# Two networks and a mixture of experts: transposes between the layers, smaller one-hot pieces, a shared last stage

## What is computed

```python
logits = xf @ w_router                       # N = 8192 rows, 8 experts
gate, eidx = jax.lax.top_k(softmax(logits), 2)
gate = gate / gate.sum(-1)
pos = cumsum(one_hot(eidx)) - 1              # place of a row in its expert, kept if < C
h = relu(expert_in @ w1[e] + b1[e])          # C = 768 rows an expert, 256 -> 1024
expert_out = h @ w2[e] + b2[e]               # 1024 -> 256
y = sum over the two choices of expert_out * gate
x = layernorm(x + y)
```

## Time and profile before

| what | us |
|---|---|
| median of 3 runs | 2886.46 |
| the profiled execution, in all | 2887.04 |
| its span | 2885.2 |
| `ssm_phase`, end of its last copy to the first load of `moe_phase` | about 2391.9 |
| from there to the end | about 493 |

### The profile page before, as it was taken

The page is one execution under the profiler, slowest core; times in us unless marked ns, Lnnn a source line. Parts: engine busy times, 40 slices in busy tenths (PEclk is TensorE's granted clock), DMA queues, the critical chain, the costliest instruction groups (busy, mean ns, idle before and its releaser), DMA issues. The chain is left out here.

```text
span 2885.2 us, 51759 instructions
## 1 busy us (share of the span) xinstructions
PE 2642.1 (92%) x16812; PEld 2403.8 (83%) x16812; DVE 2434.5 (84%) x3452; ACT 2274.4 (79%) x5161; POOL 2155.9 (75%) x2239
## 2 busy tenths in 40 slices
PE   5899999999999999999999999999999884899992
PEld 4899999999999999999999999999999874576761
DVE  1999999999999999999999999999999986112113
ACT  6999999999999999999999999999999922111113
POOL 1788888888888888888888888888888862423315
PEclk8999999999999999999999999999999986999996
DMA  1222222222222222222232222222222212323216
GB/s 59 67 75 79 78 71 79 78 69 82 71 80 77 75 76 78 73 80 70 77 81 72 79 77 75 77 78 73 80 70 79 72 51 85 81 59 99 60 43 244
DMA packets 153973, 225.73 MB, mean 78 GB/s; under 512 B 46056, under 2 KB 92776, under 8 KB 152552
## 3 DMA queue, kind: packets, MB, share of 16 engines
q1 hardware_dynamic: 131208, 188.98, 22.3%
q0 software_dynamic: 9216, 12.59, 2.5%
q10 hardware_dynamic: 13280, 20.86, 2.1%
HBM read 189.26 MB, written 33.05 MB: 77 GB/s over the span
## 5 line engine op out<-in xcount | busy, mean ns | idle before, releaser
L642 POOL TENSOR_TENSOR H<-H,CB 128x640 f32<-128x640 f32 x832 | 1236.1, 1499 | 224.0 <-DVE H L479 223.9
L479 DVE TENSOR_TENSOR_SCAN H<-DA,PM 128x704 f32<-128x704 f32 x832 | 1317.1, 1604 | 1.3 <-ACT DA L276 1.3
L394 ACT ACTIVATE DA<-DT,SM 128x160 f32<-128x160 f32 x3328 | 1115.9, 424 | 1.5 <-POOL DT L610 0.3
L664 PE MATMUL YB<-H,ID 128*128 128x160 f32 x6656 | 1050.5, 310 | 0.2 <-POOL H L642 0.2
L664 PEld LDWEIGHTS YB<-H,ID 128*128 128x128 f32 x6656 | 989.0, 192 | 16.4 <-issue 11.2
L454 DVE TENSOR_TENSOR PM<-PM,BB 128x640 f32<-128x640 f32 x832 | 678.7, 816 | 5.8 <-DMA BB<-Bd 0.7
L276 ACT ACTIVATE DA<-DA 128x2560 f32<-128x2560 f32 x208 | 485.4, 2334 | 1.7
L1121 POOL DMA_INDIRECT YA<-YS,IG x48 | 75.2, 1566 | 239.9 <-ACT YS L944 228.4
L621 POOL TENSOR_TENSOR FC<-SN,HALF 128x4 f32<-128x4 f32 x206 | 212.4, 1031 | 31.2 <-DVE SN L485 23.2
L765 PE MATMUL PZ<-WO,Z 128*80 128x256 f32 x832 | 188.5, 380 | 0.1
L1177 PE MATMUL PE<-XTE,W 128*128 128x384 f32 x512 | 169.1, 492 | 10.1 <-issue 9.2
(11 more groups left out here) (164 smaller groups left out, 3993.7 us busy)
## 6 DMA issues: line engine op xcount, KB each, us to landing
BB<-Bd SPq DMA_DIRECT2D x208, 320.0 KB, 3.4
CB<-Cd SPq DMA_DIRECT2D x208, 320.0 KB, 3.3
W<-in_w ACTq DMA_DIRECT2D x16, 1024.0 KB
XT<-in_xT SPq DMA_DIRECT2D x52, 160.0 KB, 2.2
XR<-in_xp SPq DMA_DIRECT2D x416, 20.0 KB
X2d<-VV SPq DMA_DIRECT2D x416, 20.0 KB
YA<-VV SPq DMA_DIRECT2D x416, 20.0 KB
HI<-YA SPq DMA_DIRECT2D x6, 1024.0 KB, 9.9
```

The costliest lines, as they stand in the source:

```text
L394: eng.activation(DA[:, c0:c0 + 2, :, a, m, 1:11].rearrange("p c b t -> p b c t"), DT[:, j % 2, a].rearrange("p b (c t) -> p b c t", c=2), ...
L479: eng.tensor_tensor_scan(H[:, q % 3, u], a0, DBX(u), 0.0, ALU.mult, ALU.add).then_inc(s_scan, 1)
L642: eng.tensor_tensor(h, h, cb, ALU.mult).then_inc(s_hc, 1)
L664: mm = eng.matmul(yv, ID[:], hv[:, :, :, n, 0:10], start=False, stop=n == 15)
```

## The change

Three edits, all in `moe_phase`.

1. `XT` gets a second buffer by the parity of the expert. TensorE's transposes of expert e+1 stand between the first and the second layer of e (a function `turn`), and so do VectorE's copies, behind the last eviction of e. The numbers of banks follow the new order (`turned`, `hidden`, `result`). The first layer waits for two of the three copies, and for the third ahead of its second bank.
2. The one-hot stage is done in eighths of 8 columns: tiles of 384 and 1024 columns instead of 768 and 2048, twice as many, and `LO` has half the size.
3. In the last stage `shares(b)` gives ScalarE rows 0 to 5, GpSimd row 6 and VectorE row 7 for batches 0 to 6, and 0 to 3, 4 to 5, 6 to 7 for batch 7. VectorE does its rows of batch b-1 behind the statistics of b (`normed`). SyncE's second store of a batch waits for GpSimd and VectorE.

```diff
-        XT = sb("XTE", [128, 2, 768])
+        XT = sb("XTE", [128, 2, 2, 768])
-        LO = sb("LO", [128, 2, 2, 16, 128])
+        LO = sb("LO", [128, 2, 2, 8, 128])
...
         def evacuated(n):
+            if n < 3:
+                return s_xtc, n + 1
+            e, k = (n - 3) // 22, (n - 3) % 22
+            if k < 16:
+                return (s_hr, s_hv)[k % 2], 8 * e + k // 2 + 1
             if k < 19:
-                return (s_hr, s_hv)[(k - 3) % 2], 8 * e + (k - 3) // 2 + 1
+                return s_xtc, 3 * (e + 1) + k - 15
             return s_ys, 3 * e + k - 18
+        def hidden(e, m, h):
+            return 3 + 22 * e + 2 * m + h
+        def turned(e, c):
+            return c if e == 0 else 22 * e - 3 + c
+        def result(e, c):
+            return 22 * (e + 1) + c
+        def shares(b):
+            return (6, 7) if b < B - 1 else (4, 6)
...
         def sync_program(eng):
-                for j0, j1, done, n in ((0, 5, s_x3a, 5), (5, 8, s_x3p, 3)):
-                    eng.wait_ge(done, n * (b + 1))
-                    eng.dma_start(o[:, j0:j1], rows(b)[:, j0:j1]).then_inc(s_out, 16)
+                ja, jp = shares(b)
+                eng.wait_ge(s_x3a, 6 * b + ja)
+                eng.dma_start(o[:, 0:ja], rows(b)[:, 0:ja]).then_inc(s_out, 16)
+                eng.wait_ge(s_x3p, b + jp - ja)
+                eng.wait_ge(s_x3v, b + 8 - jp)
+                eng.dma_start(o[:, ja:8], rows(b)[:, ja:8]).then_inc(s_out, 16)
...
         def vector_program(eng):
-            for c in range(4):
-                j = slice(16 * c, 16 * c + 16)
+            for c in range(8):
+                j = slice(8 * c, 8 * c + 8)
...
+            def turn(e):
+                if e >= E:
+                    return
+                if e >= 2:
+                    eng.wait_ge(s_h, 16 * (e - 1))
                 for c in range(3):
                     eng.wait_ge(s_xt, 3 * e + c + 1)
-                    eng.tensor_copy(XT[:, :, 256 * c:256 * c + 256],
-                                    bank(22 * e + c)[:].rearrange("p (a n) -> p a n", a=2)).then_inc(s_xtc, 1)
+                    eng.tensor_copy(XT[:, e % 2, :, 256 * c:256 * c + 256],
+                                    bank(turned(e, c))[:].rearrange("p (a n) -> p a n", a=2)).then_inc(s_xtc, 1)
+            turn(0)
+            for e in range(E):
                 for m in range(8):
...
+                turn(e + 1)
                 for c in range(3):
...
+            def normed(b):
+                eng.wait_ge(s_nm, b + 1)
+                for j in range(shares(b)[1], 8):
+                    eng.tensor_scalar(rows(b)[:, j], rows(b)[:, j], SD[:, b, j:j + 1], NM[:, b, j:j + 1],
+                                      ALU.mult, ALU.add).then_inc(s_x3v, 1)
...
                 for j in range(8):
                     eng.bn_aggr(MV[:, b % 4, j], BN[:, b % 4, j]).then_inc(s_mv, 1)
+                if b > 0:
+                    normed(b - 1)
+            normed(B - 1)
...
         def tensor_program(eng):
-            for e in range(E):
-                k = 22 * e
+            def turn(e):
+                if e >= E:
+                    return
                 for c in range(3):
-                    if k + c >= 8:
-                        done, n = evacuated(k + c - 8)
-                        eng.wait_ge(done, n)
+                    n = turned(e, c)
+                    if n >= 8:
+                        eng.wait_ge(*evacuated(n - 8))
...
+            turn(0)
+            for e in range(E):
                 eng.wait_ge(s_wl[e % 2], 32 * (e // 2 + 1))
-                eng.wait_ge(s_xtc, 3 * (e + 1))
+                eng.wait_ge(s_xtc, 3 * e + 2)
                 for m in range(8):
                     for h in range(2):
-                        n = k + 3 + 2 * m + h
+                        n = hidden(e, m, h)
+                        if (m, h) == (0, 1):
+                            eng.wait_ge(s_xtc, 3 * e + 3)
...
+                turn(e + 1)
                 eng.wait_ge(s_hr, 8 * (e + 1))
                 eng.wait_ge(s_hv, 8 * (e + 1))
```

More of the change, by code:

```diff
@@ L926, in scalar_program @@
             eng.wait_ge(s_rt, RT_G)
-            for c in range(4):
+            for c in range(8):
                 eng.wait_ge(s_eq[0], c + 1)
-                for j in range(16 * c, 16 * c + 16):
+                for j in range(8 * c, 8 * c + 8):
                     eng.activation(HI[:, 0, j, 0:48], HI[:, 0, j, 48:96], ACT.Copy,
@@ L937, in scalar_program @@
                         eng.wait_ge(s_y, 3 * e)
-                    eng.activation(HT[:, m, 0:384], bank(22 * e + 3 + 2 * m)[:, 0:384], ACT.Relu,
+                    eng.activation(HT[:, m, 0:384], bank(hidden(e, m, 0))[:, 0:384], ACT.Relu,
                                    bias=B1[:, e, m:m + 1]).then_inc(s_hr, 1)
@@ L949, in scalar_program @@
                 x = rows(b)
-                for j in range(5):
+                for j in range(shares(b)[0]):
                     eng.activation(x[:, j], x[:, j], ACT.Identity, bias=NM[:, b, j:j + 1],
@@ L1063, in vector_program @@
                         eng.wait_ge(s_y, 3 * e)
-                    eng.tensor_scalar(HT[:, m, 384:768], bank(22 * e + 4 + 2 * m)[:, 0:384], B1[:, e, m:m + 1], 0.0,
+                    eng.tensor_scalar(HT[:, m, 384:768], bank(hidden(e, m, 1))[:, 0:384], B1[:, e, m:m + 1], 0.0,
                                       ALU.add, ALU.max).then_inc(s_hv, 1)
+                turn(e + 1)
                 for c in range(3):
@@ L1135, in gpsimd_program @@
                 eng.wait_ge(s_nm, b + 1)
-                for j in range(5, 8):
+                for j in range(*shares(b)):
                     eng.tensor_scalar(x[:, j], x[:, j], SD[:, b, j:j + 1], NM[:, b, j:j + 1],
@@ L1151, in tensor_program @@
                     eng.wait_ge(s_gate[n], c + 1)
-                    for j in range(16):
-                        t = eng.matmul(GP, LO[:, c % 2, n, j], HI[:, n, 16 * c + j], start=(c, n, j) == (0, 1, 0),
-                                       stop=(c, n, j) == (3, 0, 15))
+                    for j in range(8):
+                        t = eng.matmul(GP, LO[:, c % 2, n, j], HI[:, n, 8 * c + j], start=(c, n, j) == (0, 1, 0),
+                                       stop=(c, n, j) == (7, 0, 7))
                     t.then_inc(s_gi, 1)
             eng.wait_ge(s_rt, RT_IX)
-            for e in range(E):
-                k = 22 * e
+            def turn(e):
+                if e >= E:
+                    return
                 for c in range(3):
-                    if k + c >= 8:
-                        done, n = evacuated(k + c - 8)
-                        eng.wait_ge(done, n)
+                    n = turned(e, c)
+                    if n >= 8:
+                        eng.wait_ge(*evacuated(n - 8))
                     eng.wait_ge(s_xe[e % 2][c], 32 * (e // 2 + 1))
@@ L1182, in tensor_program @@
                 for c in range(3):
-                    n = k + 19 + c
+                    n = result(e, c)
                     eng.wait_ge(*evacuated(n - 8))
```

37 lines of the change are left out of this document (16 added, 21 removed).

## The result

The changed kernel takes 2859.66 us (median of 4 runs, 2858.58 to 2861.19), the kernel before 2886.42 in the same comparison: a ratio of 0.9908, 95% interval 0.989 to 0.9925. The profiled execution is the longest of its four: 2861.19 us, span 2859.4, so 25.8 us of span less than before.

What follows compares the result with a forecast made beforehand. TensorE's chain was taken to bound the one-hot stage and experts, GpSimd the last stage. Terms 14.5 + 0.9 + 1.4 + 5.2 = 22.0 off 2886.46 gave 2864.5 us, range 2860.5 to 2870.

Steps and rivals of the forecast that it cites:

- Removed per boundary: 0.76 + 1.31 = 2.07: Expert layers: hidden-tile wait 0.76 and XT-copy wait 1.31 us vanish at each of seven boundaries, 14.5 us.
- those move along with the start, so I count nothing for them: Expert 0's first layer: some 4 us at half clock shift with its 0.9 us earlier start, counted as 0.
- under 2860: Sign for the whole kernel: a median under 2860 means something counted at nothing (the clock's 4 us, the stores) gave time.
- 1.4 forecast: One-hot stage in eighths: first pass starts 1.4 us earlier, 0.40 from VectorE's half tile and 0.50 per GpSimd product.
- 5.2 forecast: Last stage: rows shared by three engines finish 5.9 us earlier, less 0.7 for the DMA queue, 5.2 us.
- Rival 2: Last stage is already bound by DMA, so it gives 0: 2869.7 us; chance 0.07.
- Rival 1: Expert layers: part of the waits stays, 9.2 or 5.3 of 14.5 us remain, middle 2871.7 us; chance 0.06.
- Rival 3: Experts: TensorE's clock falls at the transposes, 2.0 us a set, 14 in all, 2878.5 us; chance 0.025.
- Rival 4: Experts: late gathered rows hold the second layer too; 5 us late each time makes 2899.5 us; chance 0.02.
- Rival 5: One-hot stage: eighths starve TensorE, 1.4 turns into -1, 2866.9 us; chance inside the forecast's 0.78.
- Rival 6: Last stage: VectorE's new row waits 1.64 us for GpSimd's L1132, 9.8 us later, 2874.3 us; chance 0.025.
- a few tenths: Expert boundaries: upper bound of the gain set at 14.5 us and a few tenths.

Runs made afterwards that it cites:

- the kernel with the split wait: Kernel before, only the wait for the last two hidden tiles moved to the second layer's eighth product: 2880.33 us, ratio 0.9972.
- the wait put back: Changed kernel with the next expert's transposes and copies moved behind the second layer's first result tile: 2867.26 us, ratio 0.9932.
- edit 1 alone: Kernel before with only the second XT buffer and the transposes and copies between the layers: 2868.51 us, ratio 0.9931.
- the 28 products: Changed kernel plus 28 unread constant-tile products ahead of the one-hot passes, last-hidden-tiles wait at the second layer's eighth product: 2859.06 us, ratio 0.99.
- all three groups: Changed kernel plus unread constant-tile products: 28 before the one-hot passes, 30 behind, 8 ahead of expert 0's second and third transpose sets: 2866.11 us, ratio 0.9926.
- the 28 and the 30: Changed kernel plus unread products, 28 before and 30 behind the one-hot passes, last-hidden-tiles wait at the second layer's eighth product: 2858.81 us, ratio 0.9898.
- all three groups with the split wait: Kernel of all three groups, with the last-hidden-tiles wait also moved to the second layer's eighth product: 2865.37 us, ratio 0.9926.

## Why the prediction was wrong

**The seven boundaries.** "Removed per boundary: 0.76 + 1.31 = 2.07" is the step that failed. The mechanism was right in every part: no wait came in place of the two, gathers, banks, copies and ScalarE were all in time. The size was off. The chain splits the time of a wait in two: the idle piece that it names, and 0.24 us that it books to the row of products behind the wait. In the kernel with the split wait the first layer keeps the wait in front of it and loses the one behind it, and still reads 20.88; with the wait put back the first layer has one behind it and none in front, and reads 20.64. So each wait is worth 0.24 us more than its idle piece, two waits a boundary, seven boundaries: 3.4 us. Shown three times, by the period of 42.67 with edit 1 alone, by 1.00 us for the 0.76 in the kernel before, and by the same 1.00 when the wait was put back.

Most of it could have been read from the page of before:

```profile
L1177 PE MATMUL PE<-XTE,W 128*128 128x384 f32 x512 | 169.1, 492 | 10.1 <-issue 9.2
L1187 PE MATMUL PE<-W,HT 128*128 128x256 f32 x768 | 167.7, 380 | 6.1 <-issue 6.1
```

A pass of the first layer lasts 0.49 us, but a layer has one every 20.88/64 = 0.33; for the second layer it is 0.38 and 0.22. Behind a running pass the next one begins 0.16 us before the first ends; a wait for the last pass takes these 0.16 in full (the ends of passes are modelled in a profile, the periods are not). The other 0.08 is the first pass behind a wait: it lasts 0.46 in the second layer of before (at 2491.39) and 0.38 in the changed kernel's (at 2488.94), and 0.56 against 0.49 in the first layer. That both are the array running empty and filling again, and not for instance the load of the first weights, no run here separates. The Trainium skill (TensorE: Matmul & The Clock Gate, Step-by-step: what each phase is for) says that the drain of a product is hidden only behind a following one that is already queued. The trace agrees in kind. The Trainium skill (TensorE: Matmul & The Clock Gate, Single matmul latency) gives a latency constant of about 166 ns at full clock, for a bf16 product; the estimate from it for fourteen waits is 2.3 us, which has the 0.16 of the rows and lacks the 0.08.

The interval of the measured ratio (2854.7 to 2864.8 us) reaches into the stated range, so it is the stages of the traces that show what was missed, more than the median.

**Expert 0.** The step "those move along with the start, so I count nothing for them" failed too. The first layer begins 0.9 earlier, as forecast. Beside that it is shorter. Over the runs, the first layer of expert 0 takes 22.90, 23.44, 23.36 and 22.87 us in the four kernels that wait for the third copy, and 21.98, 22.15, 21.56, 21.77 and 21.95 in the five profiles where it follows the transposes directly, with no warming: 23.1 against 21.9 on average, and the groups don't touch. 0.24 of the 1.3 is the wait in front of the layer; about 1.0 is clock: half speed lasts 4.0 us and more after the layer's start in the first group and 1.7 to 2.9 in the second. Why it rises sooner there (the transposes right ahead of the layer are the difference in TensorE's work) was not taken apart further. The prediction had named this as a sign: under 2860, something counted at nothing, such as the clock's 4 us, gave time too.

**The one-hot stage.** The first pass comes 1.8 us sooner, in all the runs with eighths, for 1.4 forecast: GpSimd's product of 384 columns takes 0.83 us, between my two rows of 755 and 1255 ns but below the line through them (0.92). Nothing starves TensorE. The passes took 0.9 longer in the compared pair, which is no cost of the eighths: in quarters they take 30.89, 32.06, 31.86 and 31.78 in the four profiles, in eighths 31.77, 30.86, 31.06, 31.50, 31.77 and 30.96. The profile of before is the shortest of its kind. The edit's worth over the averages: 1.8 + 0.3, the latter within their scatter.

**The last stage.** 5.2 forecast, 5.1 in the profile, 5.2 in the run of the edit alone (interval 2.0 to 7.5), and the round of VectorE as worked out. Rival 2, that DMA binds the stage already, was wrong of the kernel before and holds for the kernel after.

**The sum, mended.** 14.5 + 3.4 (0.24 a wait) + 0.9 + 1.3 (expert 0's layer) + 1.8 + 5.2 = 27.1 us; measured 26.8. Rivals 1, 3, 4, 5 and 6 did not occur; the clock in the experts was 1.00 at every set of transposes, since layers of 20.64 and 20.72 us leave no room for less. The range was too short below: it allowed "a few tenths" above 14.5, as if the idle piece of a chain were an upper bound of what a wait costs. The single edits add up to 19.9 + 3.1 + 5.2 = 28.2, each uncertain by 2.6 to 4.5, so no interaction can be seen.

## What to carry to other kernels

Price a removed wait of TensorE by the whole period with and without it, or by the same row of products once with and once without a wait in front, and not by the idle piece of the chain; here 0.76 us of idle was 1.00 us of time. A wait for the last piece of an operand can stand in front of the product that reads that piece, which gave 8.0 us here, 1.00 in each of the eight experts by the trace. And before shortening a stage's compute, run it without any: it tells at once whether the DMA is the floor.

## What the runs showed of the hardware that was not expected

- The time at half clock from the start of the one-hot passes differs between kernels that run the same 256 passes: 4.3 us before, 6.2 after, 4.3 with the eighths alone and 6.8 with the transposes alone. The kernel before and the three whose edits lie behind the passes run this stage alike, and it takes 30.89, 31.86, 31.78 and 32.06 us. With 6.2 us at half clock the passes take 31.77, at full clock throughout 28.80, so each microsecond of it costs half. Two kernels whose stage begins cold can differ there by more than 1 us though the code of the stage is the same. The Trainium skill (TensorE: Matmul & The Clock Gate, What's actually happening) says that the count of cold products differs between runs of the same kernel. No run here shows that: the only kernel with two profiles, the changed one, has 6.2 us in both.
- The clock can fall while TensorE is working: with the 28 products it fell at 2421.1, 1.7 us into the passes, after a pause of 2.4 us, and was at half until 2424.5. The profiles of two more kernels with the 28 products, of all three groups and of the 28 and the 30, show the same fall within 2 us of the start of the passes; the one of all three groups with the split wait doesn't, though its code is the same up to there (passes of 28.80 us for 30.43).
- Signals of TensorE came 2.4 and 7.0 us late in two profiles and 2.7 in a third when products that signal nobody stood between sets of transposes and their gathers. That their place matters is shown; the mechanism is open. It was not tried with a product that signals, nor with fewer than 8.
- The first network's end lies between 2390.1 and 2393.3 us in the fourteen profiles though none of its lines differs; a difference of a microsecond or two between single executions is of that size.
